# Two chained cross-attention layers in pairs of batches: Gram rows, phi G and T1 made half a pair earlier

## The chip, the cores and the metric

The kernel runs on one core of a Trainium2 chip. Its five queues are TensorE (PE), VectorE (DVE), ScalarE (ACT), GpSimd (POOL) and SyncE (SP), which only issues transfers here. The metric is the device time of one execution in microseconds.

## The reference

There are 16 batches, x and ctx are 256 x 512 each. The first layer is softmax attention from x to ctx with a residual; the second is attention without a softmax, over the channels, which allows its products to be taken in another order.

```python
# layer 0, per batch: x, ctx [256, 512]
scores = (x @ w_q.T) @ (ctx @ w_k.T).T / sqrt(512)
x1 = x + alpha * softmax(scores) @ (ctx @ w_v.T) @ w_o.T
# layer 1, per batch, on x1 and ctx as [256 channels, 512 positions]
g = g_w @ ctx + g_b ; theta = theta_w @ x1 + theta_b ; phi = phi_w @ ctx + phi_b
y = ((theta.T @ phi / 512) @ g.T).T
out = batchnorm(w_w @ y + w_b) + x1
```

## The kernel before

Every float32 operand is kept as two parts, hi (rounded, made on ACT) and lo (the rest, made on DVE), and each product is three matmuls: hi hi, hi lo and lo hi (`product`, L299 to L306; at its call the names stand in the order operand, weights). The semaphore of a lo part is what PE mostly waits for.

Batches go in pairs, p = 0 to 7. For a pair, PE makes these products, named as in the code:

- `t_tile(m)`, m = 0 to 3: tT, the weights qk = w_k, w_q folded, times ctx transposed (cT). 12 matmuls of 512 columns each.
- `gram_rows(b, i)`: G = ctx ctx^T of batch b, 8 matmuls of one part, into two PSUM banks. DVE then turns off-diagonal squares (`gram_squares`) and they go through DRAM and back over SP (`send`, `fetch`), are added (`gram_close`) and split (`gram_part`).
- `scores(b)`: 24 matmuls of 256 columns. Then maxima (DVE), exponentials (ACT), squares turned on DVE (`turn_squares`), through DRAM and back, and split as pT (`pT_part`).
- `values(b, st)`: vo = cT times ov, 12 matmuls of 512 columns, split by `vo_part`.
- `phi_gram(b)`: phi G, 6 matmuls of 258 columns; `phi_squares` on DVE, a trip through DRAM, `u_rows` and `u_part` give u.
- `delta(b, lt)`: pT times vo, 6 matmuls; `x1_rows`, `x1_part` give x1 and its parts.
- `w_g_phi(b)`: T1, u times wg, 6 matmuls of 256 columns; `t1_rows`, `t1_part` give t1.
- `theta_rows(b)`: 6 matmuls. `output(b, ct)`: 3 matmuls, then `out_rows` on DVE and a store.

The t tiles and Gram rows made inside pair p are those of pair p + 1. Each queue's order is written by hand in its `pair` function, and each works in order: PE L404 to L482, ACT L548 to L651, DVE L741 to L910, SP L245 to L285. Pair 0 is written with `first=True`, pair 7 with `last=True`, and pairs 1 to 6 are a loop. In PE's order of a pair stand: scores, values(0), values(1, 0), phi G, values(1, 1), delta, t_tile(0), theta(0), t_tile(1), T1, theta(1), t_tile(2), output(0), t_tile(3), Gram rows of batch 0, output(1), Gram rows of batch 1. On ACT the c sums (`c_sums`, L509, four activations over ctx with an accumulator) stand after tT_part(2). `cT_parts` splits the ctx of the next pair, over the operand that values has just read, so ACT waits there for `vo_done`.

PSUM has eight banks of 512 floats a partition, dealt out by the tables at L118 to L128. IDLE_PRODUCTS (9) are matmuls on zeros at the start (L318).

## Time and profile before

| | us |
|---|---|
| median of 3 runs | 397.45 (395.14, 397.45, 397.83) |
| the profiled execution | 395.43 |
| its span | 393.6 |
| PE busy | 385.4 |
| DVE busy | 291.4 |
| ACT busy | 190.8 |

The span runs from the first instruction to the last; 1.8 us of the profiled execution's time lie around it. Busy time of PE counts matmuls whose ends are modelled, so the pace is read from one start to the next.

### The profile page before, as it was taken

The page shows a single profiled execution, that of the slowest core. Times are in us where ns is not written, and L with a number is a line of the kernel's source. Part 1 is how long each engine was busy: PE and PEld are TensorE (multiplying, and loading weights), DVE is VectorE, ACT ScalarE, POOL GpSimd, SP SyncE. Part 2 cuts the span into 40 slices and gives each one's busy share as a digit, 9 for nine tenths or more (in the row PEclk, how much of TensorE's full clock was granted, in tenths as well). Part 3 has the DMA queues.
Part 4 walks back from the last instruction along what each step waited for, and adds up shares of the span by engine and source line. Part 5 has one row for each costly group of instructions (what it writes and reads, how often), then busy time and mean ns, then how long its engine had stood idle before and what let it go on. Part 6 is the DMA issues. An engine that isn't in the chain of part 4 may idle for free.

```text
span 393.6 us, 5814 instructions
## 1 busy us (share of the span) xinstructions
PE 385.4 (98%) x1967; PEld 328.6 (83%) x1967; DVE 291.4 (74%) x567; ACT 190.8 (48%) x385; POOL 1.8 (0%) x7
## 2 busy tenths in 40 slices
PE   8999999999999999999999999999999999999985
PEld 5888988889888988889888988889888988889863
DVE  5896559875698568876689567876698667876775
ACT  3464735652547335563448235563448244572441
POOL 1000000000000000000000000000000000000000
PEclk9999999999999999999999999999999999999998
DMA  8985554157650965248750966348650875016612
GB/s 244 374 311 226 151 150 113 70 171 257 203 171 2 343 176 180 100 142 285 206 167 0 312 194 185 108 122 292 185 201 0 283 219 177 13 53 188 196 45 107
DMA packets 55803, 68.13 MB, mean 173 GB/s; under 512 B 4592, under 2 KB 46320, under 8 KB 52720
## 3 DMA queue, kind: packets, MB, share of 16 engines
q1 hardware_dynamic: 55792, 67.99, 53.3%
q8 instruction: 6, 0.10, 0.1%
q14 instruction: 5, 0.04, 0.0%
HBM read 49.09 MB, written 18.87 MB: 173 GB/s over the span
## 4 chain that ended last, share of the span: by engine, by line
PE 88%; DVE 4%; DMA 3%; ACT 2%; SPq 1%; issue 1%; DVEq 0%; POOL 0%; POOLq 0%
PE bank L303 22%; PE bank L304 21%; PE bank L305 21%; PE bank L362 6%; PE bank L332 6%; PE bank L350 3%; PE bank L352 3%; PE bank L351 3%; DMA gram_moved<-gram_blocks 2%; SPq L216 1%; PE bank L319 1%; DVE xb L816 1%; DMA moved<-blocks 1%; ACT c_raw L513 1%; DVE x_lo L664 1%
## 5 line engine op out<-in xcount | busy, mean ns | idle before, releaser
L303 PE MATMUL bank<-ov_hi,c_sides 128*128 128x512 f32 x128 | 50.2, 392 | 0.0
L304 PE MATMUL bank<-ov_lo,c_sides 128*128 128x512 f32 x128 | 49.9, 390 | 0.0
L305 PE MATMUL bank<-ov_hi,c_sides 128*128 128x512 f32 x128 | 49.9, 390 | 0.0
L305 PE MATMUL bank<-c_sides,qk_lo 128*128 128x512 f32 x128 | 49.8, 389 | 0.0
L303 PE MATMUL bank<-c_sides,qk_hi 128*128 128x512 f32 x128 | 49.8, 389 | 0.0
L304 PE MATMUL bank<-c_sides,qk_hi 128*128 128x512 f32 x128 | 49.8, 389 | 0.0
L352 PE MATMUL bank<-tT_hi,xT_lo 128*128 128x256 f32 x128 | 36.2, 283 | 0.0
L351 PE MATMUL bank<-tT_lo,xT_hi 128*128 128x256 f32 x128 | 36.2, 283 | 0.0
L350 PE MATMUL bank<-tT_hi,xT_hi 128*128 128x256 f32 x128 | 36.2, 283 | 0.0
L558 ACT ACTIVATE probs<-bank,neg_max 128x256 f32<-128x256 f32 x32 | 14.9, 471 | 39.5 <-DVE neg_max L751 39.5
L493 ACT ACTIVATE x_hi<-xb 128x512 fp32r<-128x512 f32 x32 | 19.7, 632 | 28.1 <-DVE xb L816 28.0
L664 DVE TENSOR_TENSOR tT_lo<-bank,tT_hi 128x512 fp32r<-128x512 f32 x32 | 21.8, 685 | 14.1 <-ACT tT_hi L493 14.1
L305 PEld LDWEIGHTS bank<-ov_hi,c_sides 128*128 128x128 f32 x128 | 24.0, 188 | 5.2
L362 PE MATMUL bank<-c_sides 128*128 128x512 f32 (+1 forms) x128 | 28.4, 365 | 0.0
L303 PEld LDWEIGHTS bank<-c_sides,qk_hi 128*128 128x128 f32 x128 | 24.0, 188 | 5.0
L305 PEld LDWEIGHTS bank<-c_sides,qk_lo 128*128 128x128 f32 x128 | 24.0, 188 | 5.0
L304 PEld LDWEIGHTS bank<-c_sides,qk_hi 128*128 128x128 f32 x128 | 24.0, 188 | 5.0
L304 PEld LDWEIGHTS bank<-ov_lo,c_sides 128*128 128x128 f32 x128 | 24.1, 188 | 4.5
L303 PEld LDWEIGHTS bank<-ov_hi,c_sides 128*128 128x128 f32 x128 | 24.1, 188 | 4.5
L362 PEld LDWEIGHTS bank<-c_sides 128*128 128x128 f32 x128 | 23.5, 188 | 3.8
L493 ACT ACTIVATE vo_hi<-bank 128x512 fp32r<-128x512 f32 x32 | 18.9, 590 | 15.6 <-PE bank L305 15.6
L664 DVE TENSOR_TENSOR vo_lo<-bank,vo_hi 128x512 fp32r<-128x512 f32 x32 | 22.0, 686 | 5.7 <-ACT vo_hi L493 5.7
(129 smaller groups left out, 860.6 us busy)
## 6 DMA issues: line engine op xcount, KB each, us to landing
cT_raw<-ctx_t SPq DMA_DIRECT2D x8, 1024.0 KB, 5.0
xT_raw<-x_t SPq DMA_DIRECT2D x8, 1024.0 KB, 8.4
c_raw<-ctx_n SPq DMA_DIRECT2D x8, 1024.0 KB, 6.1
xb<-x SPq DMA_DIRECT2D x16, 512.0 KB, 4.9
out<-xb SPq DMA_DIRECT2D x15, 512.0 KB, 3.5
gram_moved<-gram_blocks SPq DMA_DIRECT2D x16, 256.0 KB, 6.1
gram_blocks<-gram_moved SPq DMA_DIRECT2D x64, 64.0 KB, 2.0
moved<-blocks SPq DMA_DIRECT2D x16, 256.0 KB, 2.7
```

The costliest lines, as they stand in the source:

```text
L216: sp.dma_start(dst[j * SQUARE:(j + 1) * SQUARE].rearrange("p q x a -> p q (x a)"), scratch[j].rearrange("q i n -> i q n")).then_inc(landed ...
L303: pe.matmul(dst, ahi, bhi, start=(k == 0), stop=False)
L304: pe.matmul(dst, ahi, blo, start=False, stop=False)
L305: mm = pe.matmul(dst, alo, bhi, start=False, stop=(k == k_tiles - 1))
L332: mm = pe.matmul(bank[KH * n + m][:], lhs[a][:, k, tile(m)], rhs[b][:, k, :], start=(k == 0 and a == b), stop=(k == KH - 1 and a == 1))
L350: pe.matmul(dst, x_hi, t_hi, start=(k == 0), stop=False)
L351: pe.matmul(dst, x_hi, t_lo, start=False, stop=False)
L352: mm = pe.matmul(dst, x_lo, t_hi, start=False, stop=(k == KH - 1))
L362: mm = pe.matmul(bank[GRAM_BANK[b][i]][:, i * P:], cT[0][:, k, b, tile(i)], c_sides[:, k, b].rearrange("p h s -> p (h s)")[:, i * P:], sta ...
L493: act.activation(dst, src, ACT.Identity, **more).then_inc(made, 1)
L558: e = act.activation(probs[:, b, lt], bank[SCORE_BANK[b]][:, lt * S:(lt + 1) * S], ACT.Exp, bias=neg_max[:, b, lt:lt + 1], scale=SCALE, ac ...
L664: dve.tensor_tensor(parts[1][at], src, parts[0][at].bitcast(F32), ALU.subtract).then_inc(made, 1)
```

## The change

It moves the Gram rows of the next pair from the end of a pair to the middle (behind delta, ahead of t_tile(0)), phi G of the next pair into the end of the pair (ahead of output(1)), and T1 between values(0) and values(1) of the pair that uses it. For pair 0 the Gram rows are made ahead of the t tiles, phi G stands behind the scores, and T1 behind values(1) and ahead of delta. The work on ACT, DVE and SP for these moves with them, in pairs 1 to 6 the c sums stand ahead of pT_part(1), and the tables of banks are new. The count of instructions on each engine is the same.

The banks:

```diff
-        PHI_BANK = [4, 5]
+        PHI_BANK, FIRST_PHI_BANK = [2, 3], [6, 7]
         DELTA_BANK = [[2, 3], [4, 5]]
-        TT_BANK = [6, 7, 0, 1]
-        THETA_BANK = [2, 3]
+        TT_BANK = [2, 4, 0, 7]
+        THETA_BANK = [3, 5]
         T1_BANK = [4, 5]
-        OUT_BANK = [[6, 2], [7, 5]]
-        GRAM_BANK = [[3, 4], [6, 2]]
-        WG_BANK, WG_BIAS_BANK = 5, 7
-        FIRST_T = [2, 3, 0, 1]
+        OUT_BANK = [[1, 6], [4, 5]]
+        GRAM_BANK = [[0, 1], [6, 7]]
+        WG_BANK, WG_BIAS_BANK = 4, 5
```

PE, ahead of pair 0:

```diff
-            for m in FIRST_T:
-                if m == 0:
-                    pe.wait_ge(ov_lo, KH)
-                t_tile(m)
-            for i in range(KS):
-                gram_rows(0, i)
-            pe.wait_ge(tT_lo, 3)
-            for i in range(KS):
-                gram_rows(1, i)
+            both_rows(0)
+            t_tile(0)
+            pe.wait_ge(ov_lo, KH)
+            both_rows(1)
+            t_tile(1)
+            pe.wait_ge(gram_read, 1)
+            t_tile(2)
+            pe.wait_ge(gram_read, 2)
+            t_tile(3)
```

PE, pair:

```diff
                 if first:
...
                     w_g_bias()
+                    pe.wait_ge(small_lo, 2)
+                    for b in range(2):
+                        pe.wait_ge(gram_lo, b + 1)
+                        phi_gram(b, FIRST_PHI_BANK)
+                else:
+                    pe.wait_ge(v_made, two[2])
                 for st in range(KS):
                     values(0, st)
                 if first:
+                    pe.wait_ge(v_made, two[2])
+                else:
+                    pe.wait_ge(out_made, four[0])
+                    pe.wait_ge(u_lo, p + 1)
+                    w_g_phi(0)
+                    w_g_phi(1)
+                for st in range(KS):
+                    values(1, st)
+                if first:
                     pe.wait_ge(wg_lo, 1)
                     pe.wait_ge(wg_bias_made, 1)
...
+                    pe.wait_ge(u_lo, 1)
+                    w_g_phi(0)
+                    w_g_phi(1)
                 pe.wait_ge(vo_lo, four[2])
                 pe.wait_ge(pT_lo, two[1])
                 for lt in range(KL):
                     delta(0, lt)
-                pe.wait_ge(v_made, two[2])
+                pe.wait_ge(t1_made, two[2])
...
                 if last:
                     pe.wait_ge(x1_lo, four[2])
                     theta_rows(0)
-                    pe.wait_ge(u_lo, p + 1)
-                    pe.wait_ge(x1_made, four[4])
-                    w_g_phi(0)
-                    w_g_phi(1)
                     pe.wait_ge(x1_lo, four[4])
                     theta_rows(1)
...
                 pe.wait_ge(cT_lo, two[4])
+                both_rows(0)
+                both_rows(1)
+                pe.wait_ge(x1_made, four[2])
                 t_tile(0)
...
                 t_tile(3)
+                pe.wait_ge(tT_lo, four[5])
+                for b in range(2):
+                    pe.wait_ge(gram_lo, two[b + 3])
+                    phi_gram(b)
```

ACT, pair:

```diff
                 vo_part(0, 0)
-                gram_part(0)
-                gram_part(1)
                 vo_part(0, 1)
                 pT_part(0)
+                if not first:
+                    t1_part(0)
+                    t1_part(1)
+                    if not last:
+                        c_sums(loads[32])
+                pT_part(1)
                 vo_part(1, 0)
-                pT_part(1)
                 vo_part(1, 1)
                 if not last:
                     act.wait_ge(vo_done, four[4])
                     cT_parts(loads[32])
+                if first:
+                    u_part()
+                    t1_part(0)
+                    t1_part(1)
+                    c_sums(loads[32])
```

DVE, pair:

```diff
                 pT_part(0)
+                if not first:
+                    t1_rows(0)
+                    t1_rows(1)
+                    t1_part(0)
+                    t1_part(1)
+                pT_part(1)
                 vo_part(1, 0)
-                phi_squares(0)
-                phi_squares(1)
-                pT_part(1)
                 vo_part(1, 1)
                 if not last:
                     cT_parts([two[3], two[4]])
+                if first:
+                    u_rows()
+                    u_part()
+                    dve.wait_ge(wg_bias_made, 1)
+                    t1_rows(0)
+                    t1_rows(1)
+                    t1_part(0)
+                    t1_part(1)
                 x1_rows(0)
```

SP, pair:

```diff
+                if not first:
+                    fetch_phi()
+                    next_x(0)
                 for b in range(2):
                     sp.wait_ge(blocks_made, two[b + 1])
                     send(moved[b], blocks[:, b], blocks_stored[b])
                 for b in range(2):
                     sp.wait_ge(blocks_stored[b], turned[16])
                     fetch(pT_raw[:, b], moved[b], pT_loaded[b])
```

Three places of the order, each before and after. A row is the line, the operation, what is written and read with its size, and the semaphores that it waits for; x4 is a row four times, and the names stand without their digits and buffers (t_hi is t1_hi, x_lo is x1_lo).

PE, from the last t tile made ahead of pair 0 (`c_sides` is cT, written to a bank with weights qk) to the scores of pair 0 (`tT` times `xT`), before:

```order
L305 MATMUL bank<-c_sides,qk_lo 128x512
L362 MATMUL bank<-c_sides 128x512 x4
L362 MATMUL bank<-c_sides 128x384 x4
L362 MATMUL bank<-c_sides 128x512 [waits tT_lo_made]
L362 MATMUL bank<-c_sides 128x512 x3
L350 MATMUL bank<-tT_hi,xT_hi 128x256 [waits xT_lo_made,tT_lo_made]
L351 MATMUL bank<-tT_lo,xT_hi 128x256
```

and after:

```order
L318 MATMUL bank<-c_sides,qk_hi 128x512
L319 MATMUL bank<-c_sides,qk_hi 128x512
L320 MATMUL bank<-c_sides,qk_lo 128x512
L365 MATMUL bank<-tT_hi,xT_hi 128x256 [waits xT_lo_made,tT_lo_made]
L366 MATMUL bank<-tT_lo,xT_hi 128x256
```

The 16 matmuls of the Gram rows (L362) have gone from between the last t tile and the scores, which wait for all four tT_lo.

DVE in pair 0, from the split of pT to the split of u (`phi_blocks` holds u before it is split; `t_lo` is t1's), before:

```order
L770 TENSOR_TENSOR pT_lo<-probs,pT_hi 128x512 [waits pT_hi_made]
L664 TENSOR_TENSOR vo_lo<-bank,vo_hi 128x512 [waits vo_hi_made]
L664 TENSOR_TENSOR c_sides<-cT_raw,c_sides 128x4x256 [waits cT_hi_made] x2
L816 SCALAR_TENSOR_TENSOR xb<-bank,inv_sum,xb 128x512 [waits delta_done,inv_sum_made,x0_loaded]
L816 SCALAR_TENSOR_TENSOR xb<-bank,inv_sum,xb 128x512 [waits delta_done]
L664 TENSOR_TENSOR x_lo<-xb,x_hi 128x512 [waits x1_hi_made] x2
L816 SCALAR_TENSOR_TENSOR xb<-bank,inv_sum,xb 128x512 [waits delta_done,inv_sum_made,x1_loaded]
L816 SCALAR_TENSOR_TENSOR xb<-bank,inv_sum,xb 128x512 [waits delta_done]
L664 TENSOR_TENSOR x_lo<-xb,x_hi 128x512 [waits x1_hi_made] x2
L800 SCALAR_TENSOR_TENSOR phi_blocks<-row,gram_raw,phi_blocks 128x4x32 [waits phi_blocks_loaded]
L800 SCALAR_TENSOR_TENSOR phi_blocks<-row,gram_raw,phi_blocks 128x4x32 x3
L805 TENSOR_TENSOR u_lo<-phi_blocks,u_hi 128x512 [waits u_hi_made]
```

and after, from the last phi_squares:

```order
L832 TENSOR_SCALAR v<-bank,phi_bias 128x1
L700 TENSOR_TENSOR vo_lo<-bank,vo_hi 128x512 [waits vo_hi_made] x2
L822 TENSOR_TENSOR pT_lo<-probs,pT_hi 128x512 [waits pT_hi_made] x2
L700 TENSOR_TENSOR vo_lo<-bank,vo_hi 128x512 [waits vo_hi_made] x2
L700 TENSOR_TENSOR c_sides<-cT_raw,c_sides 128x4x256 [waits cT_hi_made] x2
L841 SCALAR_TENSOR_TENSOR phi_blocks<-row,gram_raw,phi_blocks 128x4x32 [waits phi_blocks_loaded]
L841 SCALAR_TENSOR_TENSOR phi_blocks<-row,gram_raw,phi_blocks 128x4x32 x3
L846 TENSOR_TENSOR u_lo<-phi_blocks,u_hi 128x512 [waits u_hi_made]
L867 SCALAR_TENSOR_TENSOR blocks<-wg_bias,v,bank 128x256 [waits v_made,t1_done,wg_bias_made]
L867 SCALAR_TENSOR_TENSOR blocks<-wg_bias,v,bank 128x256 [waits v_made,t1_done]
```

The four rows of u and its split now stand right behind the split of the next pair's cT and ahead of x1; T1 on PE waits for that u_lo.

ACT in pairs 1 to 6, from the split of pT of batch 0 (`probs` holds pT as it landed) to that of cT, before:

```order
L493 ACTIVATE pT_hi<-probs 128x512 [waits delta_done,pT0_loaded]
L566 REGISTER_ALU [waits delta_done]
L493 ACTIVATE vo_hi<-bank 128x512 [waits vo_done]
L493 ACTIVATE pT_hi<-probs 128x512 [waits delta_done,pT1_loaded]
L493 ACTIVATE vo_hi<-bank 128x512 [waits vo_done,delta_done]
L501 ISA [waits vo_done]
L493 ACTIVATE c_sides<-cT_raw 128x4x256 [waits cT_loaded]
L493 ACTIVATE c_sides<-cT_raw 128x4x256
```

and after:

```order
L519 ACTIVATE pT_hi<-probs 128x512 [waits delta_done,pT0_loaded]
L519 ACTIVATE t_hi<-blocks 128x256 [waits t1_made] x2
L536 ISA
L539 ACTIVATE c_raw,gram_raw<-c_raw 128x512 [waits c_loaded]
L539 ACTIVATE c_raw,gram_raw<-c_raw 128x512 x3
L519 ACTIVATE pT_hi<-probs 128x512 [waits delta_done,pT1_loaded]
L603 REGISTER_ALU [waits delta_done]
L519 ACTIVATE vo_hi<-bank 128x512 [waits vo_done]
L519 ACTIVATE vo_hi<-bank 128x512 [waits vo_done,delta_done]
L519 ACTIVATE c_sides<-cT_raw 128x4x256 [waits cT_loaded,vo_done]
L519 ACTIVATE c_sides<-cT_raw 128x4x256
```

t_hi and the c sums (L539) now stand between the two pT, and so ahead of vo_hi of batch 1.

## Rows read from the trace of the kernel before

**Rows 1.** Page, part 1: busy us (share of the span) x instructions.

```profile
PE 385.4 (98%) x1967; PEld 328.6 (83%) x1967; DVE 291.4 (74%) x567; ACT 190.8 (48%) x385; POOL 1.8 (0%) x7
```

**Rows 2.** Waits of PE: us in total, times, longest us.

```profile
PE bank L303 <- DVE u_lo L805: 2.2, 2, 1.9
```

**Rows 3.** Windows, loop: stretch, its us, then busy us (x instructions), clock, DMA, GB/s.

```profile
75.00:121.00 46.00, 46.00 (x241) 39.69 (x240) 34.91 (x69) 22.61 (x47) 0.00 (x0) 1.00 0.53 172
```

**Rows 4.** Timeline of PE before pair 0: start us, us, engine, line, work, count.

```profile
38.18 3.42 PE L362 MATMUL bank<-c_sides 128*128 128x512 f32 x16
41.44 0.28 PE L350 MATMUL bank<-tT_hi,xT_hi 128*128 128x256 f32 x1
```

**Rows 5.** Timeline of ACT and DVE in the same stretch.

```profile
38.38 0.60 ACT L493 ACTIVATE tT_hi<-bank 128x512 fp32r<-128x512 f32 x1 [2.12 <-PE bank L305]
39.01 0.69 DVE L664 TENSOR_TENSOR tT_lo<-bank,tT_hi 128x512 fp32r<-128x512 f32 x1 [2.03 <-ACT tT_hi L493]
```

**Rows 6.** Timelines in pair 1: PE's first product, and after the last values.

```profile
87.92 0.28 PE L350 MATMUL bank<-tT_hi,xT_hi 128*128 128x256 f32 x1
106.04 0.39 PE L303 MATMUL bank<-vo_hi,pT_hi 128*128 128x512 f32 x1
106.30 0.60 ACT L493 ACTIVATE vo_hi<-bank 128x512 fp32r<-128x512 f32 x1 [0.39 <-PE bank L305]
110.15 1.40 DVE L816 SCALAR_TENSOR_TENSOR xb<-bank,inv_sum,xb 128x512 f32<-128x512 f32 x2
```

**Rows 7.** Timeline of DVE and PE in pair 0, around the T1 product.

```profile
70.98 1.13 DVE L800 SCALAR_TENSOR_TENSOR phi_blocks<-row,gram_raw,phi_blocks 128x128 f32<-128x128 f32 x4
72.81 0.69 DVE L805 TENSOR_TENSOR u_lo<-phi_blocks,u_hi 128x512 fp32r<-128x512 f32 x1 [0.70 <-ACT u_hi L493]
73.56 0.39 PE L303 MATMUL bank<-wg_hi,u_hi 128*128 128x256 f32 x1 [0.26 <-DVE u_lo L805]
73.79 0.28 PE L304 MATMUL bank<-wg_lo,u_hi 128*128 128x256 f32 x1
```

**Rows 8.** Timelines of DVE and PE in the last pair, to the end.

```profile
378.69 1.41 DVE L816 SCALAR_TENSOR_TENSOR xb<-bank,inv_sum,xb 128x512 f32<-128x512 f32 x2
380.28 0.39 PE L305 MATMUL bank<-x_hi,theta_w_lo 128*128 128x512 f32 x1
382.58 0.39 PE L303 MATMUL bank<-wg_hi,u_hi 128*128 128x256 f32 x1 [1.92 <-DVE u_lo L805]
385.28 0.39 PE L305 MATMUL bank<-x_hi,theta_w_lo 128*128 128x512 f32 x1
387.33 0.47 PE L303 MATMUL bank<-theta_hi,t_hi 128*128 128x512 f32 x1
388.56 0.40 PE L305 MATMUL bank<-theta_hi,t_lo 128*128 128x512 f32 x1
```

**Rows 9.** Start of the last pair; t_hi in pair 0; group of L513.

```profile
355.58 0.28 PE L350 MATMUL bank<-tT_hi,xT_hi 128*128 128x256 f32 x1
363.51 0.71 DVE L757 STREAM_TRANSPOSE blocks<-probs 128x512 f32<-128x512 f32 x1 [1.09 <-ACT probs L558]
368.89 0.63 ACT L493 ACTIVATE pT_hi<-probs 128x512 fp32r<-128x512 f32 x1 [0.67 <-DMA probs<-moved]
75.28 0.86 DVE L826 SCALAR_TENSOR_TENSOR blocks<-wg_bias,v,bank 128x256 f32<-128x256 f32 x2
75.79 0.81 ACT L493 ACTIVATE t_hi<-blocks 128x256 fp32r<-128x256 f32 x2 [1.45 <-DVE blocks L826]
L513 ACT ACTIVATE c_raw<-c_raw 128x512 f32<-128x512 f32 x32 | 19.7, 622 | 0.0
```

**Rows 10.** Window after the last product (as in rows 3); PE at the start.

```profile
391.60:391.80 0.20, 0.00 (x0) 0.00 (x0) 0.00 (x0) 0.00 (x0) 0.00 (x0) 0.52 1.22 358
1.32 4.02 PE L319 MATMUL bank<-idle 128*128 128x512 bf16 x9 [1.32 <-POOL idle L920]
6.43 1.08 PE L332 MATMUL bank<-vo_lo,tT_hi 128*128 128x512 f32 x4
```

More of the change, by code:

```diff
@@ L479, in pair @@
                     output(1, ct)
-                pe.wait_ge(out_made, four[2])
-                for i in range(KS):
-                    gram_rows(1, i)
             pair(0, first=True)
@@ L848, in pair @@
                 row_maxima(1)
+                if not first:
+                    u_rows()
                 turn_squares(1)
@@ L870, in pair @@
                     x1_part(0, lt)
+                if not last:
+                    gram_squares(0, [four[5], four[6]], two[3])
                 x1_rows(1)
-                if last:
-                    u_rows()
-                    u_part()
+                if not last:
+                    gram_squares(1, [four[7], four[8]], two[4])
                 for lt in range(KL):
                     x1_part(1, lt)
-                if not last:
-                    u_rows()
-                    u_part()
-                if first:
-                    dve.wait_ge(wg_bias_made, 1)
                 if last:
                     theta_part(0)
-                    for b in range(2):
-                        t1_rows(b)
-                    for b in range(2):
-                        t1_part(b)
                     theta_part(1)
```

206 lines of the change are left out of this document (107 added, 99 removed).

## The prediction

> **What bounds the kernel now.** I read the busy shares first. PE is busy 98% of the span, DVE 74%, ACT 48% [rows 1]. Then the windows: in a stretch of the loop PE is busy all 46.00 of 46.00 us at full clock [rows 3], so in pairs 1 to 6 nothing is to be gained by an order, only lost. Then the waits of PE: it waits in the middle of the program only for u_lo, twice, 2.2 us in all, 1.9 at most [rows 2]. The timeline shows where: 0.26 us in pair 0 [rows 7] and the rest in the last pair [rows 8]. What a new order can give is those two places and the tail behind them. What it can cost is whatever cover it takes from the waits that PE now reaches late, and those I go through one by one. A 512-column product starts about 0.23 us behind the one before it: four take 1.08 us with a last one of 0.39 [rows 10], (1.08 - 0.39) / 3 = 0.23. A 256-column one takes 0.12 by the same reading (scaled by the Gram rows and the starts in rows 7). The work itself is only moved: the same counts on each engine.
>
> **1. Start of pair 0: the Gram rows no longer cover the last t tile.** Before, 16 Gram matmuls fill 38.18 to 41.44 [rows 4] between t_tile's last product and the scores. Under that cover ACT makes the last tT_hi at 38.38 and DVE tT_lo from 39.01 to 39.70 [rows 5]. Now the Gram rows stand ahead of the tiles, PE still gets to the scores at 41.44, and the last tile ends there. The same chain follows: 38.18 to 38.38 is 0.20 for the release of ACT, 0.63 to the start of tT_lo, 0.69 for it, and 0.06 from a lo part to PE (72.81 + 0.69 = 73.50 to 73.56 [rows 7]). That is 1.58 us of waiting. After a wait the first product takes 0.11 more than it should (73.56 to 73.79 instead of 0.12 [rows 7]). Term: +1.7. ACT and DVE have the Gram copies and squares ahead of that tile, but they end some us sooner, so they add nothing. It cannot be less than 1.6, since nothing stands between; I bound it at 1.6 and 2.2.
>
> **2. T1 of pair 0 stands ahead of delta, and its u behind the split of cT.** This is the largest term. PE finishes values(1) and wants T1, which needs u_lo. On DVE the u rows stand behind cT_parts of the next pair, and cT_parts must wait on ACT for the last values product, since it overwrites what that reads. So the whole chain begins only when PE runs out of work. It can be read in two pieces. In pair 1, the last values product's slot ends where the next starts, at 106.04; ACT starts vo_hi at 106.30, and after vo_lo and the two splits of cT, DVE is free at 110.15 [rows 6]: 4.11 us. Then u_rows, u_hi on ACT, u_lo, PE: 70.98 to 73.56 in pair 0 [rows 7], 2.58 us. Together 6.69, and 0.11 for the first product: +6.8. The trip of phi through DRAM is shorter than that wait: phi is turned before the values products are half done, and SP is through with pT by then. So it is DVE's order and not a transfer that ends last. Behind the waiting T1 on PE stands everything; ACT and DVE wait too, and so nothing is done early in those 6.7 us that PE could use later, because PE has no other wait in the pair to win back. Bounds: 6.0 (if ACT starts the splits of cT a little sooner) and 8.0 (if the phi trip is late by one us).
>
> **3. The old waits for u_lo.** In pair 0 PE sat idle 0.26 before 73.56 [rows 7]; a product's last 0.16 (0.39 - 0.23) lies over the next one's start, so the wait was 0.42, and with the slow product behind it -0.5. In the last pair T1 is gone from the tail. Before, PE ends theta(0) at 380.51 (380.28 + 0.23), resumes at 382.58, and its last product starts at 388.56 and its slot ends at 388.79 [rows 8]. Now theta(1) is next and needs x1_lo of batch 1. Its two x1 rows take 378.69 to 380.10 [rows 8]; then x1_hi on ACT and x1_lo on DVE, the same kinds of step as in rows 5: 0.03 + 0.63 + 0.06 + 0.69 + 0.06 gives 381.57. So a wait of 1.1 us stands where 2.1 stood. theta(1) then ends at 381.57 + 0.11 + 6 x 0.227 = 383.04. Its theta_lo is ready 1.8 us behind it (385.28 + 0.23 = 385.51 to 387.33 [rows 8]); output(0) covers 1.36 of that, and output(1) ends at about 383.04 + 1.8 + 1.36 + 0.1 = 386.3. Before it was 388.79, of which 12 x 0.12 = 1.4 was T1, work that is only moved. Net: 386.3 - (388.79 - 1.4) = -1.1. Bounds -0.6 and -1.6.
>
> **4. The clock.** PE will stand still for 6.7 us, longer than anywhere in this trace. What the trace shows of this: after the last product (388.56 + 0.40) the granted clock falls to half in the window at 391.6 [rows 10], 2.65 us later. A wait of 2 us in the last pair left it at 1.00. At the start, from rest, products run slow from 1.32: nine take 4.02 us, 0.45 each, and at 6.43 the pace is 0.23 [rows 10]. So it takes up to 5.1 us of work to come back from 1.2 to 2.4 GHz, and 40 to 50% of that is lost: 2.0 to 2.6, and as a part of those 5.1 us was waiting I take 2.1. Bounds: 0 (the clock stays up) and 3.3 (it stays down two us longer).
>
> The Trainium skill (TensorE: Matmul & The Clock Gate, Part 1: The HAM clock gate) says that the array has just two levels, 1.2 and 2.4 GHz, that it falls back after idling and comes back only after being busy for a time, and that the ramp is below 1% of a typical kernel's span. By that last figure the term would be an estimate of up to 3.9 us. No mid-kernel fall is in this trace, so only the rows at both ends bear on it.
>
> **5. The loop.** New cover, pair by pair: scores have phi G and output(1), 1.4 + 1.4 us, ahead of them for a chain of 1.6 (item 1), so they don't wait. The tight place is vo_lo of the last values product ahead of delta(1). From the start of the last pair at 355.58, turn_squares of batch 1 ends at 364.22 (8.64 in), and pT_hi of batch 0 starts 4.67 later, at 13.31 [rows 9]. The new order hangs t1 and the c sums on that: pT_hi and pT_lo (two steps like those of rows 5, 1.27 together), t1_rows and both t_hi 75.28 to 76.60, 1.32 [rows 9], four c sums of 0.61, 2.45 [rows 9], gives 18.4 for pT_hi(1). Then pT_lo starts 0.63 later, and DVE does it and two vo_lo, 1.9: 20.9. PE wants it after 106.04 - 87.92 = 18.12 [rows 6] (scores and values, with 12 products of T1 in place of those of phi G) plus delta(0), 12 x 0.227 = 2.72: 20.84. So it is even: 0.06 us late, if the pT pieces land as in that pair. Each pair would lose 0 or about 0.06 + 0.06 + 0.11 = 0.2. Over six pairs I take +1.0, with 0 and +3.6 (0.6 a pair, if the load of x, now issued ahead of the squares, delays pT by 0.4) as bounds. A pair takes (355.58 - 87.92) / 6 = 44.61 [rows 6, 9], and the old u_lo wait costs nothing in it.
>
> **Sum**, against the profiled execution: 395.43 + 1.7 + 6.8 - 0.5 - 1.1 + 2.1 + 1.0 = 405.4. The profiled execution is 2.0 below the median of the runs, and the four executions (three runs and this one) average 396.46, 1.0 above it. I add 1.0: **406.4**.
>
> **The rivals.**
> - A, the forecast: both new waits, the clock falls, the loop is about even: 406.4.
> - B, the clock does not fall in the 6.7 us, or at once returns. For it: the 2.1 us wait of the last pair shows 1.00. Against: the fall 2.65 us after the last product. 406.4 - 2.1 = 404.3.
> - C, the loop breaks: delta(1) waits about 0.6 us in each of six pairs, from the point where pT of batch 0 lands over 4.7 us behind the turned squares. For it: item 5 is even on paper. Against: elsewhere pT lands sooner. 406.4 + 2.6 = 409.0.
> - D, the other side: the wait of item 2 does not arise. Its place is T1 of pair 0; it decides from where u_lo is ready within 1 us of the end of values(1), because the splits of cT and u_rows get done under values(1). Then items 2 and 4 fall away: 395.43 + 1.0 + 1.7 - 0.5 - 1.1 + 1.0 = 397.5, no change; with the loop's term at zero 396.5. For it: ACT is 48% and DVE 74% busy. Against: the semaphore that says the operand was read comes only with the last product.
> - E, no net loss from the loop and short waits (lower bounds in items 1, 2, 3 and 5, the clock stays up): 395.43 + 1.0 + 1.6 + 6.0 - 0.5 - 1.6 = 401.9.
>
> **How the numbers follow.** A 0.62, B 0.13, C 0.15, D 0.04, E 0.06. A measurement here tells about 1% (4 us) from no change: below 393.5 is faster (0.02, D with a gain in the tail and more), 393.5 to 401.4 the same (0.06: D and a third of E), above it slower (0.92). The range leaves out D and the far end of C: 401.8 to 410.0.
>
> **What would show it.** PE's waits should have two new rows: 1.6 us for tT_lo ahead of the scores of pair 0, and 6.7 us for u_lo at w_g_phi in pair 0, with the granted clock at 0.5 in part of the 5 us behind it. In the last pair the wait for u_lo is gone and one of about 1.1 for x1_lo is in its place. The distance between Gram rows of successive pairs shows the loop: 44.61 if it is even, up to 44.9 in A, over 45.1 in C. A wait for u_lo in pair 0 under 5 us, or for a transfer in place of DVE, would make item 2 wrong; a period below 44.6 would make the reading of a full PE wrong.

## The result, and the profile after

The changed kernel takes **404.71 us** (median of 6 runs, 403.8 to 405.71); the kernel before, beside it, 396.92 (6 runs, 395.14 to 397.83). The ratio is 1.0199, 95% interval 1.0168 to 1.023: slower by about 2%; whether by more than 2% stays open. The profiled execution took 403.80 us with a span of 402.0, that of before 395.43 and 393.6, so 8.4 us are to be found between the two traces.

The page after, part 1 (busy us, share of the span, x instructions) and the row of the granted clock from part 2:

```profile
PE 386.7 (96%) x1967; PEld 329.9 (82%) x1967; DVE 291.6 (73%) x567; ACT 187.6 (47%) x385; POOL 1.8 (0%) x7
...
PEclk9999997899999999999999999999999999999999
```

The same instructions as in [rows 1]; PE's share fell from 98 to 96% because the span grew. The clock has a dent in the slices from 60 to 80 us, which before had not.

PE's waits after (us in total, times, longest us), against the one row in [rows 2]:

```profile
PE bank L318 <- DVE u_lo L846: 6.6, 1, 6.6
PE bank L365 <- DVE tT_lo L700: 1.4, 1, 1.4
...
PE bank L318 <- DVE x_lo L700: 0.9, 1, 0.9
PE bank L318 <- DVE theta_lo L876: 0.3, 1, 0.3
```

Four places, two in the first pair and two in the last. I go through them in the order of time.

**Start of pair 0.** Timeline of PE around the first product of the scores (start, us, engine, line, work, count, idle before and its releaser):

```profile
42.81 0.39 PE L365 MATMUL bank<-tT_hi,xT_hi 128*128 128x256 f32 x1 [1.41 <-DVE tT_lo L700]
```

The last product of the t tile starts at 41.02. I call the 0.23 us from one start to the next a product's slot; this one ends at 41.25, so the scores are 1.56 us late, and 0.11 more for the slow first product: **+1.67**. Before, the Gram rows filled this time [rows 4, 5].

**T1 of pair 0.** SP, DVE and ACT while PE stands still, then PE:

```profile
58.94 1.73 SPq L215 DMA_DIRECT2D phi_blocks<-phi_moved  x4
62.53 0.60 ACT L519 ACTIVATE vo_hi<-bank 128x512 fp32r<-128x512 f32 x1 [2.12 <-PE bank L320]
63.16 0.69 DVE L700 TENSOR_TENSOR vo_lo<-bank,vo_hi 128x512 fp32r<-128x512 f32 x1 [2.03 <-ACT vo_hi L519]
64.10 2.36 DVE L700 TENSOR_TENSOR c_sides<-cT_raw,c_sides 128x1024 fp32r<-128x1024 f32 x2 [0.26 <-ACT c_sides L519]
66.38 1.13 DVE L841 SCALAR_TENSOR_TENSOR phi_blocks<-row,gram_raw,phi_blocks 128x128 f32<-128x128 f32 x4
68.20 0.69 DVE L846 TENSOR_TENSOR u_lo<-phi_blocks,u_hi 128x512 fp32r<-128x512 f32 x1 [0.69 <-ACT u_hi L519]
```

```profile
62.10 0.39 PE L320 MATMUL bank<-ov_hi,c_sides 128*128 128x512 f32 x1
69.04 0.55 PE L318 MATMUL bank<-wg_hi,u_hi 128*128 128x256 f32 x1 [6.55 <-DVE u_lo L846]
...
71.53 0.41 PE L320 MATMUL bank<-wg_hi,u_lo 128*128 128x256 f32 x1
```

The slot of the last values product ends at 62.33, T1 starts at 69.04: **+6.71**. The rows say what the 6.7 us are: vo's splits, 2.4 us of cT's splits, then the rows of u with no idle time ahead of them (66.38 has no bracket), u_hi, u_lo. Phi's row was fetched at 58.94 and is not what ended last.

**The clock.** Windows of the same stretch (us, busy PE, PEld, DVE, ACT, POOL, then the granted clock):

```profile
62.00:65.00 3.00, 0.49 (x3) 0.07 (x1) 1.59 (x2) 2.47 (x3) 0.00 (x0) 1.00 0.00 1
65.00:66.00 1.00, 0.00 (x0) 0.00 (x0) 1.00 (x2) 0.01 (x1) 0.00 (x0) 0.83 0.00 0
66.00:72.00 6.00, 2.96 (x13) 2.99 (x14) 2.71 (x8) 1.04 (x2) 0.00 (x0) 0.50 0.00 0
72.00:73.00 1.00, 1.00 (x4) 0.78 (x4) 0.85 (x3) 0.51 (x2) 0.00 (x0) 0.76 0.00 0
```

The granted clock falls to half (1.2 GHz) at about 65.7, 3.2 us after the last product's end, and is back at about 72.5, 3.5 us after T1's start. T1's twelve products take 69.04 to 71.74, 2.70 us in place of 1.43, and the first two of delta lose 0.35: **+1.6**.

**The loop.** Gram rows start at 122.17, 166.81, 211.44, 256.07, 300.71 and 345.34: a period of 44.63, so even; before it was 44.61: **+0.1** over six pairs. The tight place in one of the pairs (it starts at 232.52), ACT and DVE, then PE's first product of delta(1):

```profile
245.11 0.63 ACT L519 ACTIVATE pT_hi<-probs 128x512 fp32r<-128x512 f32 x1 [0.57 <-DMA probs<-moved]
...
250.06 0.61 ACT L519 ACTIVATE pT_hi<-probs 128x512 fp32r<-128x512 f32 x1
...
251.31 1.28 DVE L700 TENSOR_TENSOR vo_lo<-bank,vo_hi 128x512 fp32r<-128x512 f32 x2
```

```profile
253.35 0.39 PE L318 MATMUL bank<-vo_hi,pT_hi 128*128 128x512 f32 x1
```

vo_lo is done at 252.59, PE comes at 253.35: 0.76 us between them, about 0.7 to spare. Read the same way, pairs 1 to 6 have 0.36, 0.48, 0.58, 0.66, 0.58 and 0.57 to spare (0.10 us is what PE needs from a vo_lo's end, as e10 shows).

**The tail.** PE in the last pair; rows 8 have it before:

```profile
391.11 0.39 PE L320 MATMUL bank<-x_hi,theta_w_lo 128*128 128x512 f32 x1
392.37 0.50 PE L318 MATMUL bank<-x_hi,theta_w_hi 128*128 128x512 f32 x1 [0.87 <-DVE x_lo L700]
394.99 0.39 PE L320 MATMUL bank<-theta_hi,t_lo 128*128 128x512 f32 x1
395.68 0.47 PE L318 MATMUL bank<-theta_hi,t_hi 128*128 128x512 f32 x1 [0.30 <-DVE theta_lo L876]
```

What PE loses here is 1.03 + 0.10 ahead of theta(1) and 0.46 + 0.08 ahead of output(1), 1.67 us; before it was 2.68 (2.07 of it for u_lo): **-1.0**. In pair 0 the old u_lo wait of 0.52 [rows 7] is gone: **-0.5**.

The sum: 1.67 + 6.71 + 1.6 + 0.1 - 1.0 - 0.5 = +8.6. The loads of the start came 0.25 us sooner in this execution (the first product on cT at 27.05, before at 27.30): +8.3 against 8.4 measured. So the time is found. What is only argued so far is why each piece is there, and what takes its place if it goes.

### The profile page after: what moved, and what is told of

Its sections match the earlier page's. It is cut to its first block, busy times and chain, and to the rows that moved or that the text cites. A ratio compares the mean times of both kernels' runs of the same rounds, so it can differ in the third digit from the quotient of the medians.

```text
span 402.0 us, 5804 instructions
## 1 busy us (share of the span) xinstructions
PE 386.7 (96%) x1967; PEld 329.9 (82%) x1967; DVE 291.6 (73%) x567; ACT 187.6 (47%) x385; POOL 1.8 (0%) x7
## 4 chain that ended last, share of the span: by engine, by line
PE 93%; DVE 3%; ACT 1%; DMA 1%; issue 0%; DVEq 0%; SPq 0%; ACTq 0%
PE bank L318 23%; PE bank L319 23%; PE bank L320 23%; PE bank L377 6%; PE bank L347 5%; PE bank L365 4%; PE bank L366 4%; PE bank L367 4%; DMA cT_raw<-w_q 1%; DVE c_sides L700 1%; DVE xb L883 0%; DVE xb L857 0%; DVE tT_lo L700 0%; DVE x_lo L700 0%; ACT x_hi L519 0%
## 5 line engine op out<-in xcount | busy, mean ns | idle before, releaser
L519 ACT ACTIVATE tT_hi<-bank 128x512 fp32r<-128x512 f32 x32 | 19.0, 594 | 29.3 <-PE bank L320 29.3
L377 PE MATMUL bank<-c_sides 128*128 128x512 f32 (+1 forms) x128 | 27.5, 365 | 0.0
```

The source lines that it names most:

```text
L377: mm = pe.matmul(bank[GRAM_BANK[b][i]][:, i * P:], cT[0][:, k, b, tile(i)], c_sides[:, k, b].rearrange("p h s -> p (h s)")[:, i * P:], sta ...
L519: act.activation(dst, src, ACT.Identity, **more).then_inc(made, 1)
```

## The experiments

**My theory:** the loss is PE's waits in the first pair, set by the order on DVE (6.7) and by the bare last t tile (1.7), plus the clock that falls in the longer one (1.6); the loop itself is sound. **Rivals:** the phi trip ends last and DVE's order only looks guilty; the slow products behind the wait have another cause than the clock; the loop would break elsewhere. Each run does all the work of the reference; e3, e10 and e12 add work whose result nobody uses. The ratios are to the kernel before, measured beside each; its median was 396.0 to 397.0.

**e1, u first.** On DVE and ACT, the first pair's u ahead of the splits of cT.

```diff
                 vo_part(1, 1)
+                if first:
+                    u_rows()
+                    u_part()
                 if not last:
                     cT_parts([two[3], two[4]])
                 if first:
-                    u_rows()
-                    u_part()
```

> In the first pair only, u's eight rows and the two splits of u (VectorE's and ScalarE's) stand ahead of the two splits of cT, on both engines. If VectorE's order sets the 6.7 us wait for u_lo ahead of T1 (its values splits end at 63.8 us into the changed kernel's span, and u costs 2.6 us from there), u_lo is there at about 66.4 in place of 69.0: the wait falls to about 4.1 us and the kernel is 2.7 us faster than the changed one, about 402.0, or 401.5 if the clock comes back sooner too. The clock should still fall, since the gap is still over 3.2 us. If the trip of phi's row over the DMA queue ended last, the wait stays at 6.7 us and the time within 0.5 us of the changed kernel's 404.7.

Measured: 401.54 us, ratio 1.015 (1.0126 to 1.0175). PE's wait:

```profile
PE bank L318 <- DVE u_lo L847: 3.9, 1, 3.9
```

T1 starts at 66.45 in place of 69.04. So DVE's order set the end of the wait, and the trip's rival falls. This shows 2.6 us of the 6.7; that the other 3.9 are vo's splits and u itself is read from the trace. The clock fell here too, at about 66.9, after T1 had started, and the products lost 1.6 us.

**e2, T1 between the two deltas.** On PE alone:

```diff
                     values(1, st)
+                pe.wait_ge(vo_lo, four[2])
+                pe.wait_ge(pT_lo, two[1])
+                for lt in range(KL):
+                    delta(0, lt)
                 if first:
 ...
                     w_g_phi(0)
                     w_g_phi(1)
-                pe.wait_ge(vo_lo, four[2])
-                pe.wait_ge(pT_lo, two[1])
-                for lt in range(KL):
-                    delta(0, lt)
```

> In the first pair T1 stands on TensorE behind the first sample's delta and ahead of the second's; nothing else is moved. If T1 only waits for VectorE to come to u, delta(0)'s 2.7 us run inside the wait: T1 starts at the same 69.0 us, its wait falls from 6.7 to about 4 us. Delta(1) then waits for the T1 rows to be read out of its banks, which is new and costs about 0.8 us. So the kernel is about 1.9 us faster than the changed one, 402.8; 4.5 us faster at most if the shorter gap (3.9 us) also keeps the clock from falling (1.6 us more, and no wait for the banks). If T1's inputs come later than what stands there says, for instance because u needs something that delta(0) delays, no gain: 404.7.

Measured: 403.68 us, ratio 1.02 (1.0179 to 1.022). The waits came as expected, PE:

```profile
69.28 0.36 PE L318 MATMUL bank<-wg_hi,u_hi 128*128 128x256 f32 x1 [3.84 <-DVE u_lo L846]
...
71.64 0.80 PE L318 MATMUL bank<-vo_hi,pT_hi 128*128 128x512 f32 x1 [0.57 <-DVE blocks L867]
```

2.7 us of the wait are gone, 0.9 came back at the banks. The time did not follow: 402.8 was forecast, and by the ratios nothing was gained (1.02 against 1.0199). The gap of 3.8 us did not keep the clock up. It fell at about 70.7, 1.4 us *after* PE had begun again, stayed at half until 77.5, and took 2.5 us (0.3 in delta(1)'s first product, 2.2 spread over the rest of it and the first Gram rows) in place of 1.6. Delta could be pulled into the wait, yet the clock took 0.9 of the 1.8 us back, and the profiled execution is only 0.2 us shorter.

**e3, products without use in the wait.** 26 bf16 products of a zero tile ahead of the wait for u_lo; they add work that the kernel throws away.

```diff
                     pe.wait_ge(wg_bias_made, 1)
+                    for _ in range(26):
+                        pe.matmul(bank[0][:], idle[:, 0:P], idle[:], start=True, stop=True)
                     pe.wait_ge(u_lo, 1)
```

> The wait for u_lo is left as it is, but 26 products without use (bf16, 512 columns, 0.216 us each, 5.6 us together) fill it on TensorE, into a PSUM bank that is free then. Nothing else is changed, T1 starts at 69.0 us as before. If the low clock is what makes the products behind the wait slow (0.213 instead of 0.12 us), they go at full pace now, the granted clock doesn't fall in the trace and the kernel is 1.6 us faster than the changed one: 403.1. If the slow pace behind the wait is something else (weights, operands that come late), or if the fall is harmless because DVE and ACT set the pace there, the time stays within 0.4 us of 404.7 or is longer by what the products overrun.

Measured: 402.65 us, ratio 1.017 (1.0153 to 1.0187); 2.1 under the changed kernel by the medians, 1.2 by the ratios. Windows of the filled wait and of what is behind it:

```profile
62.00:69.00 7.00, 6.42 (x30) 2.77 (x28) 4.60 (x8) 3.12 (x4) 0.00 (x0) 1.00 0.00 1
69.00:75.00 6.00, 5.75 (x31) 5.03 (x32) 3.50 (x8) 3.92 (x12) 0.00 (x0) 1.00 0.01 3
```

The clock stays at 1.00, and T1's products are 0.12 apart again. So the slow pace behind the wait is the clock.

**e4, the bias product as cover.** In the first pair, w_g_bias (which waits for two t tiles only) ahead of the scores.

```diff
+                if first:
+                    pe.wait_ge(ww_scaled, 1)
+                    pe.wait_ge(g_bias_made, 1)
+                    pe.wait_ge(tT_lo, 2)
+                    w_g_bias()
                 pe.wait_ge(tT_lo, four[4])
                 pe.wait_ge(xT_lo, two[1])
                 scores(0)
 ...
-                    w_g_bias()
```

> In the first pair the small bias product (1.1 us) stands ahead of the scores instead of behind them, so it runs in the time in which TensorE waits for the fourth t tile's split. If the 1.67 us at the start are the split's time with no work beside it, 0.6 to 1.1 us of them go: 403.6 to 404.1. If something else holds the scores there (the loads of x, the scaled weights), the time stays at 404.7 within 0.3 us.

Measured: 403.99 us, ratio 1.0195 (1.0178 to 1.0212), so at the lower edge by the medians and nothing by the ratio. The trace has the 1.1 us: the wait for tT_lo is gone from the list, 0.57 us are left ahead of the scores in place of 1.67. But delta(1) of pair 1 is now 0.5 us late, which it wasn't in the changed kernel, and the clock was low from 64.3 to 74.5 in this execution, so that the products lost 2.8 us. Two of the four runs had a mean clock of 0.986 and two of 0.990; the latter are 1 us faster on the average. So what a fallen clock costs differs from run to run by as much as this edit gives.

**e5, T1 behind both deltas.** u first as in e1, T1 ahead of the Gram rows in banks 6 and 7, and delta(1) no longer waits for T1's banks.

```diff
-        T1_BANK = [4, 5]
+        T1_BANK, FIRST_T1_BANK = [4, 5], [6, 7]
 ...
                 for lt in range(KL):
                     delta(1, lt)
+                if first:
 ...
+                    w_g_phi(0, FIRST_T1_BANK)
+                    w_g_phi(1, FIRST_T1_BANK)
 ...
                 both_rows(0)
+                if first:
+                    pe.wait_ge(t1_made, 2)
                 both_rows(1)
```

> In the first pair T1 stands behind both samples' delta, ahead of the Gram rows, in the two banks that are free there, and u stands ahead of the splits of cT as in the run with u first; delta(1) need not wait for T1's banks. By my theory u_lo (66.4 us into the span) comes while TensorE is still at delta (5.4 us from 62.5 on, to 67.9), so no wait of several us is left in the first pair and the clock doesn't fall: 4.1 us better than u first with its 3.9 us wait, less some 0.5 for small waits, and 1.6 for the clock; against the changed kernel's 404.7 about 5.5 to 7 us less, 397.7 to 399.2. If the wait at T1 hides another that would take its place (delta for its vo_lo, the Gram rows for their banks), it is still above 401.

Measured: 400.26 us, ratio 1.0083 (1.0055 to 1.011). The clock stays up and the long wait is gone, but five new ones stand in its place, 3.4 us with their slow first products, where I had allowed 0.5; so the time is above the 397.7 to 399.2 forecast. The two largest:

```profile
PE bank L318 <- DVE vo_lo L704: 0.9, 1, 0.9
...
PE bank L318 <- DVE xb L861: 0.8, 1, 0.8
```

The first pair's DVE is behind by what u and T1's rows take, and PE meets it at t_tile(1) (1.1), theta(1) (0.4), phi G (0.25), the scores of pair 1 (0.5) and its delta(1) (1.1).

**e8, T1 put back.** The first pair's T1 behind t_tile(1), as before the change, in two halves of bank 1; u behind x1 of the first sample, T1's rows behind tT_part(1), the c sums and the load of c later. All else as changed.

```diff
                 pe.wait_ge(x1_made, four[4])
                 t_tile(1)
+                if first:
 ...
+                    pe.wait_ge(gram_read, 3)
+                    pe.wait_ge(u_lo, 1)
+                    for b in range(2):
+                        w_g_phi(b, bank[1][:, b * L:(b + 1) * L])
                 pe.wait_ge(x1_lo, four[4])
                 theta_rows(1)
```

> The first pair's T1 is put back where it stood before the change, behind the second t tile, in two halves of one free bank; u and T1's rows go back behind the x1 sums, and the load of c behind them. The pairs behind and the first pair's bare fourth t tile are as in the changed kernel. If T1's place alone makes the loss, the 6.7 us and the clock's 1.6 us go and 0.5 to 1.0 us come as small new waits (before had 0.5 there): 396.4 to 397.5, that is no slower than before, since 1.7 us of loss at the start stand against 1.0 to 1.1 of gain in the last pair. If the loop's own order cost anything (rival: it is a loop loss spread over all pairs), the time would stay above 399.

Measured: 398.13 us (10 runs), ratio 1.0035 (1.0019 to 1.005). This undoes 1.64 of the 1.99% in one stroke: 6.5 us, net of new waits, are T1's place in the first pair with what had to move along (u, T1's rows, the c sums). The rest is more than I forecast: 0.35% slower than before, where I had expected none. PE's timeline has the largest new wait in pair 1, ahead of delta(1):

```profile
112.98 0.39 PE L324 MATMUL bank<-vo_hi,pT_lo 128*128 128x512 f32 x1
114.32 0.47 PE L322 MATMUL bank<-vo_hi,pT_hi 128*128 128x512 f32 x1 [0.95 <-DVE vo_lo L708]
```

1.34 us from start to start where 0.23 belongs. Two smaller ones are new as well: 0.85 us ahead of phi G at the end of pair 0 (for gram_lo) and 0.3 at the scores of pair 1.

**e9, T1 put back and two covers.** e8 with e4's edit, and the scores of every pair wait for the fourth tT_lo only at the product that reads it:

```diff
                     for k in range(KH):
+                        if whole is not None and lt == 0 and k == KH - 1:
+                            pe.wait_ge(tT_lo, whole)
 ...
-                pe.wait_ge(tT_lo, four[4])
+                pe.wait_ge(tT_lo, four[3])
                 pe.wait_ge(xT_lo, two[1])
-                scores(0)
+                scores(0, four[4])
```

> The run with T1 put back, and two covers for the fourth t tile's split: the first pair's bias product stands ahead of the scores, and the scores wait for the fourth split only at the product that reads it (each pair). The bias product took the bare time at the start down by 1.1 us in its own run, the inner wait should take the last 0.5 and nothing in the pairs that have cover anyway. 1.6 us less than T1 put back: about 395.2, which is 0.3% faster than the kernel before. Rival: the inner wait costs TensorE's queue something in each pair (0.06 us, eight times), or the fourth split sets the scores' end: then no better than 396.4.

Measured: 396.53 us (12 runs), ratio 0.9987 (0.9973 to 1.0002). 1.6 less than e8, as expected, though the time is that of the rival (396.4) and not the 395.2 forecast, since e8 was itself above its forecast. The rival's reason doesn't hold: a later pair takes 44.63 us as before, so the inner wait costs nothing there. The kernel is level with the kernel before, not measurably faster. The wait in pair 1 is still there, now 1.45 us.

**e10, more work for ACT in the loop.** In pairs 1 to 6, two activations into a tile that nobody reads then, between the c sums and the second pT split.

```diff
                         c_sums(loads[32])
+                        for n in range(2):
+                            act.activation(row[:, ROW_GAMMA:ROW_GAMMA + H].bitcast(mybir.dt.bfloat16)[:, n * H:(n + 1) * H],
+                                           qk[0][:, n, :].bitcast(F32), ACT.Identity)
                 pT_part(1)
```

> In pairs 1 to 6 ScalarE does two more activations of 512 columns (about 0.6 us each, from and to tiles that nobody waits for) behind the sums of c and ahead of the second sample's pT split. My reading of the changed kernel's loop is that the splits for delta(1) are done 0.7 to 0.8 us before TensorE comes to them: 1.2 us more should then give a wait of 0.4 to 0.5 us in each of six pairs, with 0.1 more for the restart, so 2.4 to 3.6 us in all: 407.1 to 408.3, and a period of 45.1 in place of 44.63. If the loop has more slack than that (ScalarE's work isn't on the way to delta(1)), nothing changes: 404.7, period 44.63. If it has none, the full 1.2 us show in each pair: 412.

Measured: 409.32 us, ratio 1.0304 (1.0281 to 1.0328): +4.6 us, above my range. DVE and PE in the pair that lost least:

```profile
256.30 1.28 DVE L703 TENSOR_TENSOR vo_lo<-bank,vo_hi 128x512 fp32r<-128x512 f32 x2
```

```profile
257.06 0.39 PE L320 MATMUL bank<-vo_hi,pT_lo 128*128 128x512 f32 x1
257.68 0.47 PE L318 MATMUL bank<-vo_hi,pT_hi 128*128 128x512 f32 x1 [0.23 <-issue]
```

vo_lo ends at 257.58 and PE goes on at 257.68, so this is the chain that sets delta(1). The two activations put the second pT split back by 1.04 us; PE is 0.39 late here, so 0.65 us were to spare, as read above. In the six pairs it is 1.04, 0.72, 0.45, 0.39, 0.54 and 0.66 late, each with 0.08 more: 4.3 in all. So pairs 2 to 6 have 0.3 to 0.65 us of slack here, and pair 1 none: my range took the largest for all. In the profiled execution the fallen clock of the first pair cost 2.4 us too, 0.8 more than in the changed kernel's.

**e11, phi's row sent sooner.** In e9, phi's row comes back late in pair 1. The fetch on SP and the rows of u that need it on DVE, pair 1:

```profile
93.17 1.81 SPq L215 DMA_DIRECT2D phi_blocks<-phi_moved  x4
```

```profile
98.31 1.14 DVE L853 SCALAR_TENSOR_TENSOR phi_blocks<-row,gram_raw,phi_blocks 128x128 f32<-128x128 f32 x4 [1.57 <-DMA phi_blocks<-phi_moved]
```

In pair 2 that row has no wait. The edit, on DVE (and SP's send of phi ahead of store(0)):

```diff
                 out_rows(0, 0)
-                out_rows(0, 1)
-                tT_part(3, four[8])
                 phi_squares(0, two[3])
                 phi_squares(1, two[4])
+                tT_part(3, four[8])
+                out_rows(0, 1)
```

(in the first pair only.)

> The version with T1 put back and both covers has one wait left that I had not expected: 1.4 us in pair 1 ahead of the second sample's delta. There phi's row comes back at 98.3 us, while in pair 2 it is there before VectorE wants it; everything behind it on VectorE, the probabilities' trip too, comes 1.5 us late. It was sent at 90.8, about 1.4 us later in its pair than pair 1's own row for pair 2 was sent, since VectorE in pair 0 has u and T1's rows more to do ahead of the turned squares of phi. Here the first pair turns phi's squares ahead of the fourth t tile's split and of one output part (1.2 us sooner), and SyncE sends them ahead of the first store. If that is the cause, the wait in pair 1 falls from 1.4 us to under 0.3 and the kernel is 1.2 us faster than the run with covers: 395.3, or 0.4% under the kernel before. If the late trip comes from what shares the DMA queues then (the x load, the stores), the wait stays and nothing is won: 396.5.

Measured: 396.37 us, ratio 1.0002 (0.9989 to 1.0015). A miss: the row was sent 1.5 us sooner and fetched at the same time, since SP's two stores stand ahead of the fetch. The wait in pair 1 stayed: 1.47 us, in e9 1.45.

**e12, u first and products without use.** e1 with 16 idle products as in e3.

> U first, as in that run, with 16 products without use (3.5 us) in its wait of 3.9 us, so that the clock stays up. If the two losses of the first pair are two terms that add (the wait by VectorE's order, 2.7 us of it, and the fallen clock, 1.6 to 2.0), this is 4.3 to 5.1 us under the changed kernel: 399.6 to 400.4. If the clock's loss had been inside the same time as the wait's (T1's rows and delta late for another reason), no more than u first alone, 401.5.

Measured: 400.05 us, ratio 1.0094 (1.0075 to 1.0113), 4.7 under the changed kernel by the medians, 4.2 by the ratios. The two terms add, 2.6 for the order and 1.6 for the clock; its trace has 0.6 us of new wait at delta(1) of pair 1 as well. Such a wait is in every version with a shorter first pair: 0.1 in e2 and e3, 0.5 in e4, 0.6 here, 1.1 in e5, 1.2 in e8, 1.45 in e9.

**e13, the fetch ahead of both stores.** e11, and on SP in the first pair:

```diff
                     send(phi_moved, phi_blocks[:], phi_stored)
+                    sp.wait_ge(phi_stored, turned[32])
+                    fetch(phi_blocks[:], phi_moved, phi_loaded)
                 sp.wait_ge(out_made, four[2])
                 store(p, 0)
```

> Sending phi's row sooner changed nothing: it left at 89.35 in place of 90.82 us, but the fetch still went out at 92.93 (93.17 before), behind SyncE's two stores of pair 0, the second of which waits for the last output part on VectorE (it ends at 92.0). Against the scores that is 0.8 us ahead of the first exp, in pair 2 it is 2.1 us ahead. Here the fetch stands ahead of both stores, so it goes out at about 91.8; nothing else is changed against that run. If the fetch's place on SyncE's queue sets it, phi is back 1.1 us sooner, the wait in pair 1 falls from 1.4 us to 0.2 to 0.4, and the kernel takes 395.3 us, 0.25 to 0.3% under the kernel before. If the bytes of the stores and the x loads on the DMA engines set it (rival), they are only behind it now, the probabilities' trip gets their share, and the wait stays above 1 us: 396.4.

Measured: 398.91 us (6 runs), ratio 1.0068 (1.0045 to 1.009), slower, and above both what I forecast and the rival. Two waits of the profiled execution (400.83 us), SP's and PE's:

```profile
SPq L201 <- DMA out<-xb: 1.8, 1, 1.8
```

```profile
PE bank L330 <- DVE vo_lo L720: 3.0, 1, 3.0
```

The load of x may only go once the store is done, it stands on SP ahead of the sends of the probabilities, and those are what delta(1) hangs on. They are slow on their way too: the fetches go out 4.65 us behind the first send (98.95 to 103.60), in a loop pair of the changed kernel 3.1 (238.49 to 241.60). And the clock fell here, after a wait of only 3.0 us: at 115.2, 0.4 us after PE had begun again at 114.78, until 118.6, and the products lost 1.4 us. Three of the six runs have a mean clock of 0.995 or 0.996 and take 399.5 to 400.8 us, three have 0.999 or 1.0 and take 398.0 to 398.4. If a low mean clock is this same fall, the waits alone cost about 1.8 us against e11, and the fallen clock about 1.8 more in half of the executions.

**e14, the fetch between the stores.** e13 with store(0) back in front of the fetch.

> The run with the fetch ahead of both stores took the wait for phi away, but its two stores then left 3.5 us later, pair 1's load of x stands behind them on SyncE (it overwrites what the first store reads) and waited 1.8 us more, and the two sends of the probabilities behind that load went out at 98.95 in place of 95.67: delta(1) of pair 1 waits 3.0 us. Here the first store goes out as soon as its rows are there (90.7), the fetch stands between the two stores. If SyncE's queue is the cause of both losses, the fetch goes out at about 91.6, the sends at 95.7 as before, the wait in pair 1 is 0.2 to 0.7 us in place of 1.4, and the kernel takes 395.5 us, 0.2% under the kernel before (hardly more than five rounds tell). If it is the bytes on the DMA engines (half a MB of the second store now beside the sends), the wait stays at 1.4 us or more: 396.4 or above.

Measured: 396.24 us, ratio 1.0004 (0.9992 to 1.0015). Phi is there in time (the rows of u have no wait), but ACT then waits for the probabilities:

```profile
103.90 0.63 ACT L538 ACTIVATE pT_hi<-probs 128x512 fp32r<-128x512 f32 x1 [2.14 <-DMA probs<-moved]
```

DVE turns the second sample's squares at 97.68 in place of 99.37 in e9, and pT lands only 0.6 us sooner (103.90 for 104.52; 0.16 of both is an earlier start of the loads). Delta(1) is 0.98 us late in place of 1.45. The fetches of the probabilities go out 4.8 us behind the first send (95.88 to 100.70), against 3.1 in the loop, and SP waits 1.9 us there for the sends to land. So SP's order was one part of it. The other is that the sends land late; that this is the DMA's own traffic (the second store, the load of x, both now beside the sends) is my reading, and none of those transfers was moved by itself. By the time nothing is won: 396.24, against the 395.5 forecast.

## Why the prediction was right, and where its sizes were off

The forecast was 406.4, measured 404.7: within its range, and 1.7 too long. The total is nearer to rival B (404.3, the clock stays up) and doesn't decide between the two; the traces do, and they show case A. By its own steps:

- **Item 1, +1.7:** measured 1.67. The chain of [rows 5] could be carried over piece by piece, since the same four steps follow one another and nothing else is released there. e4 and e9 show that it is a matter of cover: 1.1 of it go with the bias product in front, and with the inner wait too 0.2 is left.
- **Item 2, +6.8:** measured 6.71. The reason, "DVE's order and not a transfer that ends last", is shown by e1; that the whole wait goes with T1's place is shown by e5 and e8. The two pieces from two different pairs (4.11 and 2.58) held to 0.1 us.
- **Item 3, -0.5 and -1.1:** measured -0.5 and -1.0. No run undid the last pair's part alone; it rests on the traces, which all have it alike.
- **Item 4, +2.1:** measured 1.6, mis-sized by 0.5. I took up to 5.1 us to come back, from the start of the program, and had it back after 3.5 us. But the term isn't a fixed one: the traces have 1.6 (changed kernel), 2.8 (e4) and 2.4 (e10) for waits of 6.6 us, and 1.6 (e1), 2.5 (e2) and 1.4 (e13) for waits of 3.9, 3.8 and 3.0 us. That it is the clock is shown by e3 and e12. The Trainium skill (TensorE: Matmul & The Clock Gate, Part 1: The HAM clock gate) puts a ramp below 1% of a typical kernel's span; by that the traces agree, 1.4 to 2.8 us of some 400.
- **Item 5, +1.0:** measured 0.1. The failed step is the place of the first pT split, taken from the last pair at 13.31 us into the pair. In the loop it is at 245.11 - 232.52 = 12.59, in the six pairs at 12.59 to 12.88, and the chain behind it ran as worked out (7.48 us from there to the end of vo_lo, 7.6 worked out). What was even on paper had 0.7 us of slack in that pair, and e10 shows that it is this chain and about this much. That the term came so near was in part luck; see below.
- **The offset, +1.0:** the profiled execution was 0.9 below the median again.

0.5 + 0.9 and the 0.25 us of sooner loads make up the 1.7, to rounding.

**Item 5, and the luck in it.** [rows 9] was the only pair from which I read the place of the first pT split, and nothing in the prediction says why it should stand for the loop. What I held against rival C, "elsewhere pT lands sooner", is wrong for the old trace: there pairs 1 to 6 have this split at 14.4 to 15.4 us into the pair, and with those numbers the same sum gives about 10 us over six pairs. SP and ACT in one of these pairs before (it starts at 221.75), then SP in the pair from 232.52 after:

```profile
226.84 3.75 SPq L216 DMA_DIRECT2D gram_blocks<-gram_moved  x8
230.81 0.93 SPq L211 DMA_DIRECT2D moved<-blocks  x2
236.91 0.63 ACT L493 ACTIVATE pT_hi<-probs 128x512 fp32r<-128x512 f32 x1 [2.39 <-DMA probs<-moved]
```

```profile
238.49 3.07 SPq L210 DMA_DIRECT2D moved<-blocks  x2
```

The sends of the probabilities stood behind the fetches of the Gram trip and went out 9.06 us into the pair; in the changed kernel that trip has left this place, and they go out at 5.97, as soon as the first squares are turned (5.94). In the old last pair, which has no loads of later pairs beside it, the same Gram fetches were through by 5.8. So the loop is sound because the Gram trip moved away from ahead of the sends, a step that the prediction doesn't have. This is read from the traces; no run moves the trip alone.

Of the rivals, B (the clock stays up) is refuted by the windows, 0.50 from 66 to 72 us, and all six runs of the changed kernel have a mean clock of 0.989 or 0.990; in e13, behind a wait of 3.0 us, half of the executions do keep it up. C is refuted by the even period; D by the wait itself; E had the loop right, and its 1.6 for item 1.

The gain that the reordering could bring is in the tail (1.0) and in the cover it frees; what it asks is that the first pair not follow. e9 keeps the tail and gives away 1.45 us in pair 1 and 0.85 in pair 0 (for gram_lo), and it is level with the kernel before (0.9987, an interval that just takes in 1). No version measured is faster than the kernel before.

## What to carry to other kernels

When a step is moved half a stage ahead, look first at the round that has no half stage before it: there the operands aren't ready, and the wait for them is the whole chain from the engine that runs dry, read from rows of the old trace and added up. Price a wait of several us on TensorE at more than its length: the clock can fall in it, and cover won afterwards (e2) can be lost to a clock that falls later. When a number of the old trace is to stand for the new order, ask which queue set it there, and whether what stood ahead on that queue is still there: the same split lay at 13.3 in one pair, at 14.4 to 15.4 in the others, and at 12.6 to 12.9 after the change. And on a queue that one engine issues in order, moving one transfer ahead (e13) moves all behind it back: count the waits of what it is moved past.

## What was not expected of the hardware

- The granted clock can fall after TensorE has begun again: in e2 at about 70.7 us with the restart at 69.28, in e1 at 66.9 with the restart at 66.45, in e13 at 115.2 with the restart at 114.78. From the end of the last product to the fall it was 2.3 us (e4), 3.2 (changed kernel), 3.4 (e13), 4.3 (e1), 5.0 (e10) and 5.2 (e2), and it stayed low for 10.2, 6.8, 3.4, 3.4, 6.8 and 6.8 us. The windows of e4 at the fall and at the return:

```profile
64.00:65.00 1.00, 0.00 (x0) 0.00 (x0) 1.00 (x2) 0.47 (x1) 0.00 (x0) 0.64 0.00 0
...
74.00:75.00 1.00, 1.00 (x4) 0.80 (x4) 0.75 (x1) 0.94 (x5) 0.00 (x0) 0.74 0.00 0
```

- The same kernel can keep or lose the clock behind the same wait: in e13, with 3.0 us, three runs of six lost it by their mean clock, at a price of about 1.8 us.
- Products without use kept the clock at 1.00 through a wait (e3, 0.8 us of it left bare; e12, 0.4 us). e3 is 2.1 us under the changed kernel by the medians and 1.2 by the ratios, e12 1.5 and 2.2 under e1, at no cost that the traces show.
